# Who takes the positive part and the residual in the output stage of a graph network kernel: VectorE and ScalarE before, ScalarE and GpSimd after

## The reference, cut to what matters

```python
def _L1_gnn_ref(x, W, a, edge_index):
    Wx = (x @ W.T).reshape(n, HEADS, HEAD_DIM)
    ...                                    # e: attention logit of each edge, m: maximum over a destination
    ex = jnp.exp(e - m[dst])
    denom = jax.ops.segment_sum(ex, dst, num_segments=n)
    alpha = ex / denom[dst]
    out = jax.ops.segment_sum(alpha[..., None] * h_src, dst, num_segments=n)
    return jax.nn.elu(out.reshape(n, OUT_DIM))
...
h = jnp.maximum(_layernorm(x, axis=-1), 0.0)
x = x + _L1_gnn_ref(h, L1_gnn_W, L1_gnn_a, edge_index)
```

## Time and profile before

| | us |
|---|---|
| median of 3 runs | 2282.91 (2282.8 to 2283.63) |
| the profiled execution, its own time | 2282.86 |
| its span, first to last instruction | 2281.1 |
| mean granted TensorE clock, share of full speed | 0.954 |
| output stage: first transpose starts | 2248.79 |
| output stage: last finish (L1211) ends | 2276.77 |

### The profile page before, as it was taken

The page is one execution under the profiler, slowest core; times in us unless marked ns, Lnnn a source line. Parts: engine busy times, 40 slices in busy tenths (PEclk is TensorE's granted clock), DMA queues, the critical chain, the costliest instruction groups (busy, mean ns, idle before and its releaser), DMA issues.

```text
span 2281.1 us, 63259 instructions
## 1 busy us (share of the span) xinstructions
PE 2003.9 (88%) x15342; PEld 1794.7 (79%) x15343; DVE 1989.7 (87%) x3852; ACT 1361.5 (60%) x3479; POOL 1641.3 (72%) x1735
## 2 busy tenths in 40 slices
PE   1899999999999999999559999999899999899996
PEld 0788888787788878878558888888888888888885
DVE  7889998998899989989568888888888888888886
ACT  2566666666666666666644555555555555555555
POOL 4777777777777777777527777777777777777772
PEclk9999999999999999999777999999999999999998
DMA  7444444444444444443023333333333333333322
GB/s 208 116 134 133 136 130 128 132 133 134 132 136 128 131 131 133 135 131 111 5 69 62 60 59 58 59 59 59 58 59 58 59 58 58 60 58 59 59 59 67
DMA packets 338046, 214.22 MB, mean 94 GB/s; under 512 B 169981, under 2 KB 304502, under 8 KB 337990
## 3 DMA queue, kind: packets, MB, share of 16 engines
q0 software_dynamic: 53248, 112.57, 20.2%
q1 hardware_dynamic: 282190, 99.72, 17.4%
q10 hardware_dynamic: 2552, 1.28, 0.2%
HBM read 201.37 MB, written 10.29 MB: 93 GB/s over the span
## 4 chain that ended last, share of the span: by engine, by line
POOL 49%; issue 22%; DMA 13%; DVE 8%; PE 4%; ACT 3%; POOLq 1%; SPq 0%; DVEq 0%; ACTq 0%
POOL msg L624 26%; POOL ring_h L590 22%; DMA ring_h<-h_dram,meta_g 10%; DMA msg<-wx_dram,meta_g 3%; DVE sums L1011 2%; DVE seg_max L1016 2%; ACT banks L756 2%; PE sums L1263 1%; DVE onehot L995 1%; DVE prod L1162 1%; POOL ring_h L614 1%; POOL diff L612 1%; DVE diff L929 0%; PE banks L1340 0%; DMA nodes<-in_x 0%
## 5 line engine op out<-in xcount | busy, mean ns | idle before, releaser
L624 POOL DMA_INDIRECT msg<-wx_dram,meta_g x832 | 791.8, 952 | 293.1 <-issue 246.7
L590 POOL DMA_INDIRECT ring_h<-h_dram,meta_g x832 | 788.6, 948 | 261.3 <-issue 248.1
L1263 PE MATMUL sums<-onehot,prod 128*128 128x128 f32 x3296 | 679.8, 290 | 14.2 <-issue 6.1
L1263 PE MATMUL sums<-onehot,wgt 128*128 128x128 f32 x3296 | 665.9, 285 | 0.0
L1263 PEld LDWEIGHTS sums<-onehot,prod 128*128 128x128 f32 x3296 | 528.4, 202 | 47.6 <-issue 47.0
L1263 PEld LDWEIGHTS sums<-onehot,wgt 128*128 128x128 f32 x3296 | 529.2, 202 | 0.0
L725 ACT ACTIVATE acc<-sums 128x1022 f32 x410 | 419.5, 1023 | 0.3
L756 ACT ACTIVATE banks<-ring_h 128x512 f32<-128x512 f32 x208 | 125.1, 602 | 319.8 <-DMA ring_h<-h_dram,meta_g 319.8
L1272 PE MATMUL banks<-beta_ident,msg 128*128 128x128 f32 x1664 | 242.6, 290 | 79.8 <-DVE msg L1034 78.5
L1283 PEld LDWEIGHTS sums<-neg_ident,seg_max 128*128 128x128 f32 x1664 | 219.0, 192 | 99.8 <-issue 99.8
L1272 PEld LDWEIGHTS banks<-beta_ident,msg 128*128 128x128 f32 x1664 | 203.8, 193 | 108.4 <-issue 92.4
(11 more groups left out here) (165 smaller groups left out, 2804.9 us busy)
## 6 DMA issues: line engine op xcount, KB each, us to landing
msg<-in_edge_attr SPq DMA_DIRECT2D x207, 256.0 KB, 3.0
flags<-flag_dram SPq DMA_DIRECT2D x52, 512.2 KB
ring_h<-h_dram,meta_g POOLq DMA_INDIRECT x832
msg<-wx_dram,meta_g POOLq DMA_INDIRECT x832
window<-wx_dram SPq DMA_DIRECT2D x832, 2.0 KB
wx_dram<-msg SPq DMA_DIRECT2D x13, 272.0 KB, 2.4
nodes<-in_x SPq DMA_DIRECT2D x6, 512.0 KB, 6.8
h_dram<-acc SPq DMA_DIRECT2D x12, 256.0 KB
```

The costliest lines, as they stand in the source:

```text
L590: pool.indirect_dma_start(hg[:, s % HRING, b, :], None, h_dram, bass.IndirectOffsetOnAxis(ap=meta_g[:, s, b:b + 1], axis=0)).then_inc(L0[" ...
L624: pool.indirect_dma_start(msg[:, s, b, :], None, wx_dram, bass.IndirectOffsetOnAxis(ap=meta_g[:, s, b:b + 1], axis=0)).then_inc(L1["gather ...
L1263: ins = pe.matmul(where[:, j, bass.ds(off, P)], what[:, slot, b, :], onehot[:, s, b, :], start=(b == 0), stop=(b == GB - 1), skip_group_ch ...
```

## The change

VectorE loses L1198 in its seven even batches. The positive part is taken by ScalarE in nine batches (0, 1, 3, 4, 6, 7, 9, 10, 12) and by GpSimd in four (2, 5, 8, 11), and GpSimd adds the residual in all 13. The semaphore `fin_pos` is gone; `fin_cut` orders GpSimd's add behind its own max, and VectorE waits for `fin_sum` in every batch, in `finish1` and before the mult that writes a slot of `ring_h` again.

```diff
+        POOL_RELU = (2, 5, 8, 11)
+        ACT_RELU = tuple(b for b in range(NBAT) if b not in POOL_RELU)
...
             def residual_sum(b):
-                if b % 2:
-                    pool.wait_ge(fin_above, b // 2 + 1)
-                    tiles = above[:, b % FIN, :].rearrange("p (t d) -> p t d", d=D)
-                    pool.tensor_tensor(tiles, tiles, nodes[:, b * GB:(b + 1) * GB, :], ALU.add).then_inc(fin_sum, 1)
+                t, r = extent(b)
+                tiles = above[0:r, b % FIN, 0:t * D]
+                if b in POOL_RELU:
+                    pool.wait_ge(fin_y, b + 1)
+                    if b >= FIN:
+                        pool.wait_ge(fin_out, b - FIN + 1)
+                    pool.tensor_scalar(tiles, ring_h[0:r, b % HRING, 0:t * D], 0.0, None, ALU.max).then_inc(fin_cut, 1)
+                    pool.wait_ge(fin_cut, POOL_RELU.index(b) + 1)
+                else:
+                    pool.wait_ge(fin_above, ACT_RELU.index(b) + 1)
+                pool.tensor_tensor(tiles.rearrange("p (t d) -> p t d", d=D), tiles.rearrange("p (t d) -> p t d", d=D),
+                                   nodes[0:r, b * GB:b * GB + t, :], ALU.add).then_inc(fin_sum, 1)
...
-                if b % 2:
+                if b in ACT_RELU:
                     if b >= FIN:
                         act.wait_ge(fin_out, b - FIN + 1)
                     act.activation(above[0:r, b % FIN, 0:t * D], y, ACT.Relu).then_inc(fin_above, 1)
...
-                    dve.wait_ge(fin_pos, (b - HRING) // 2 + 1)
+                    dve.wait_ge(fin_sum, b - HRING + 1)
...
-                if b % 2 == 0:
-                    if b >= FIN:
-                        dve.wait_ge(fin_out, b - FIN + 1)
-                    dve.wait_ge(fin_y, b + 1)
-                    dve.scalar_tensor_tensor(above[0:r, b % FIN, 0:t * D].rearrange("p (t d) -> p t d", d=D),
-                                             y.rearrange("p (t d) -> p t d", d=D), 0.0,
-                                             nodes[0:r, b * GB:b * GB + t, :], ALU.max, ALU.add).then_inc(fin_pos, 1)
...
-                if b % 2:
-                    dve.wait_ge(fin_sum, b // 2 + 1)
-                else:
-                    dve.wait_ge(fin_pos, b // 2 + 1)
+                dve.wait_ge(fin_sum, b + 1)
```

More of the change, by code:

```diff
@@ L282, in gnn_kernel @@
         fin_exp = sem("fin_exp")
-        fin_pos = sem("fin_pos")
+        fin_cut = sem("fin_cut")
         fin_above = sem("fin_above")
```

## The result

| | before | after |
|---|---|---|
| median of 22 runs, us | 2282.95 (2281.48 to 2284.92) | 2279.11 (2277.39 to 2283.07) |
| profiled execution, its own time / span | 2282.86 / 2281.1 | 2278.70 / 2276.9 |
| first transpose of the stage starts | 2248.79 | 2247.70 |
| last finish starts, with its length: ends | 2276.77 | 2272.96 |
| output stage, from the one to the other | 27.98 | 25.26 |

The ratio is 0.9984, with a 95% interval of 0.9979 to 0.9990: 3.7 us less (2.3 to 4.8), within 0.2%. The forecast was 5.3 us less. The time lies in the range; the likeliest case was the wrong one.

A forecast was written before the change was run, and what follows sets the result against it. VectorE was taken to bound the output stage. Removing L1198 saves 6.03 us; minus 0.75 for GpSimd at the end, minus 0.3 for the clock, plus 0.3 in the tail: 5.3 less, 2277.5 us, range 2275.9 to 2279.9.

The forecast's parts named there:

- the likeliest case: Whole program 5.3 us shorter, 2277.5 us, 0.24% faster; own range 2276.3 to 2278.6, chance 0.66.
- two rivals: Output stage: GpSimd bounds it (2279.3 us, chance 0.12), or TensorE's half clock does (2279.6 or 2278.7 us, chance 0.17).
- GpSimd's max, M = 0.65: Price in us of GpSimd's 128x512 max in the output stage; GpSimd keeps up with VectorE while it is below 0.95.
- GpSimd becomes the bound: Output stage: max priced like an add, 1.28 us; three batches cost GpSimd 5.07 against VectorE's 4.74; 2279.3 us, chance 0.12.
- the sum: Output stage: 6.03 us saved up to finish(10), 0.75 given back at the end, 0.3 lost to clock, 0.3 gained in tail.
- VectorE at 1.58 to 1.59 per step, each L1198 worth 1.00: Output stage: odd steps take 1.58 us, even ones 2.58; the only difference is L1198, 1.00 us of path each time.
- TensorE's clock, 0.3 booked against the change: Output stage transposes: one partly exposed half-clock stretch costs 0.3 us (0 to 0.7); more of them a rival, chance 0.17.
- step 0: First even VectorE step: removing L1198 saves nothing, as recip(2) waits for TensorE's transposes anyway, idle for 0.53 us.
- ScalarE hidden, with 0.35 to spare: Output stage: three batches cost ScalarE 4.39 us, below VectorE's 4.74, so its added work costs nothing.
- Contention of finish with GpSimd, 0: Output stage: finish, with one input from PSUM, stays at 0.68 us beside GpSimd; rival of stretched finishes, slower, chance 0.03.
- The tail, 0.3: Last stores: batch 10's store is out of the way earlier, counted as 0.3 us gained, from 0 to 0.7.
- The threshold: The 0.2% line, a gain of 4.6 us, is crossed near a GpSimd max price of 1.0 us.

The follow-up runs named there:

- the run shows 1.48: Changed kernel plus extra GpSimd operations on scratch buffers, eleven before the output stage and three after the last finish, to price them; 2283.56 us.
- the run with an operation of 1.27: Changed kernel with GpSimd's four max operations replaced by a multiplication with a tile of ones; 2277.64 us, ratio 0.9977, stage 24.40 us.
- the run with the copy: Changed kernel with GpSimd's four max operations replaced by a copy of the same tile; 2280.12 against 2287.08 us, ratio 0.9971, stage 22.20 us.
- the run with four instances back: Changed kernel with max and add of batches 2, 5, 8, 11 back on VectorE in one instruction; 2284.14 against 2287.08 us, ratio 0.9987.
- the last four comparisons: Repeats: changed kernel (0.9996), all positive parts on ScalarE (0.9966), that without ScalarE's second pass, twice (0.9984, 0.9954), each against the kernel before.

## Why the prediction was right or wrong, point by point

The time came out in the range because the range had been drawn around two rivals, and one of them is what happened. The forecast's own case did not.

- **GpSimd's max, M = 0.65: the step that failed.** It takes 1.48 to 1.50, and lies outside even the range that I had given it (0.48 to 1.28). I had taken the two-input operation as the upper end, in the belief that one input can't cost more than two, and the cast as the nearest row. That is little nearer: the run shows 1.48. The rival "GpSimd becomes the bound" is what happened, with its order of waits, at a chance of 0.12. That its time is so near (2279.3 against 2279.11) is in part luck. It was priced with M = 1.28, and for that M it was right: the run with an operation of 1.27 shortened the stage by 3.58 us, and the rival had 3.57. With 1.49 the stage and tail gave 3.1, and the medians differ by 3.8, because the rest of the program, which the change doesn't touch, took less as well (1.09 less in the profile).
- **What it did to the sum.** Finish(10) starts 21.84 after the first transpose instead of 26.51 before, so 4.67 of the 6.03 were left. Finish(0) starts 4.17 after it, 1.00 earlier than the sum has it (2253.96 - 2248.79 = 5.17), for the reason in the next point but one. The ten steps behind it take 2.36 longer than in the sum: 1.93 by the waits of finish(2), (5) and (8) (1.13 + 0.40 + 0.40), the rest in hundredths per step. At the end GpSimd takes back more: from finish(10) to the end of the last finish 3.42 instead of the 2.22 of the prediction and the 1.47 of before. 4.67 - 1.95 = 2.72, the measured difference of the stages.
- **VectorE at 1.58 to 1.59 per step, each L1198 worth 1.00:** right as sizes. Shown by the changed kernel's free steps, by the run with the copy, and by the run with four instances back (1.04 each). What the prediction did not see is that 0.2 of the 1.00 is a wait for GpSimd's add.
- **TensorE's clock, 0.3 booked against the change:** nothing was lost by it, and the sum had missed its other side. In the profile before, transposes of the first batches ran at the half clock, and recip(2) waited 0.53 for them; the prediction took that wait as given, and so counted step 0 as worth nothing. In the changed kernel's profile all transposes ran at the full clock. That made finish(0) 1.00 earlier than in the sum, but GpSimd took it back. What it means for the comparison: at the full clock the stage before would have been up to 0.5 shorter, so of the 2.72 between 2.2 and 2.7 belong to the change. Of the 14 profiles three have stretches at the half clock: before and with four fused instances in the first batches and once more later, and with the multiplication once, for batches 6 and 7. The early ones began 1.3 and 1.0 us after the first transpose, before the first L1198 (2.16) or its like (5.49) had started, so the fused instruction did not bring them about. What does is not shown. A recip waited 0.5 to 0.7 where such a stretch was exposed, so the range of 0 to 0.7 was sound.
- **ScalarE hidden, with 0.35 to spare:** right for nine batches. With all 13 it is the bound at 1.64, as its rows say.
- **Contention of finish with GpSimd, 0:** right, 0.68 to 0.69 beside a GpSimd that never rests. L1198, which the prediction named as the other kind, shows it with 0.72 to 1.02 beside an add.
- **The tail, 0.3:** 0.39 measured (4.33 to 3.94).
- **The threshold.** I wrote that the line of 0.2% (4.6 us) is crossed near M = 1.0, and gave GpSimd as the bound 12 in 100. No run has an M near 1.0. By stage and tail, 6.2 us were gained with 0.61, 3.9 with 1.27 and 3.1 with 1.49, so the line lies somewhere between 0.61 and 1.27; by its ratio alone, 0.23% (0.14 to 0.32), the run with 1.27 can't be put on either side of it. The chance was too low: it rested on one extrapolated row, of another operation.

## What to carry to other kernels

An operation moved to GpSimd needs a price from a row of the same kind, at the same size. If the trace has none, the chance of the case must be that of a guess, and the point from which it decides (here 0.95 us for three batches of 4.74) should be compared with the whole spread of GpSimd's rows. Where two engines stand within a few per cent of the bound, work moved to the third pays only until that one is full: here ScalarE could take all 13 positive parts (2.2 us better than giving four to GpSimd). And a stage of 30 us inside 2280 is judged by its own two marks in the profile, which repeat to 0.02 us where the total spreads by 5; but each profile is first to be checked for stretches at the half clock, since one of them can move the stage by half a microsecond or more.

## What the runs showed of the hardware

- On GpSimd, 128x512 f32 from SBUF to SBUF: an operation with a constant 1.48 to 1.50 us (0.52 for 128 elements), with two constants 1.94, two tensors 1.27, in place or not (but 1.09 to 1.10 for L612 of the middle stage, which stays unexplained), a copy 0.61. One input can cost more than two.
- A VectorE instruction with both inputs in SBUF does not go on beside an add of GpSimd: it ended 0.54 or 0.55 us after the add in nine rows of nine, at 0.72 to 1.02 us instead of 0.69. One with an input in PSUM (finish) kept its 0.68 to 0.69 beside the same adds.
- In the last four comparisons every version took 3340 to 3420 us instead of 2280, with a mean granted clock of 0.79 instead of 0.95. The output stage was not slower at all (25.27 against 25.26 us); the time went into the edge sweeps, with longer waits on all engines; ScalarE's longest, 660 and 454 us in total, have a releaser that the profile doesn't show. What set it off is not shown.
